# Softmax attention on one core: row sums moved into the maxima's PSUM banks, a third bank for scores, one maximum per instruction, and a new order within each tile

## The reference, cut to what matters

```python
out = softmax(q @ k_txt.T * SCALE, masked) @ v_txt + softmax(q @ k_img.T * SCALE) @ v_img
```

## Time and profile before

| | |
|---|---|
| time of the runs, median of 3 | 3357.7 us |
| time of the profiled execution | 3349.82 us |
| its span in the profile | 3347.8 us |
| attention, from the first score to the last `scale` | 906.7 to 2568.7 us |
| TensorE busy in the span | 3063.8 us (92%) |
| VectorE, ScalarE, GpSimd busy | 61%, 48%, 41% |

### The profile page before, as it was taken

How to read it: one execution, slowest core, us unless ns; L and a number is a source line. 1 busy time by engine, 2 the same in 40 slices (tenths; PEclk the granted TensorE clock), 3 DMA queues, 4 the chain that set the end, 5 groups by cost and what they waited for, 6 DMA issues and landing times. The chain is left out here.

```text
span 3347.8 us, 49752 instructions
## 1 busy us (share of the span) xinstructions
PE 3063.8 (92%) x15756; PEld 1888.5 (56%) x15756; DVE 2053.6 (61%) x3425; ACT 1606.9 (48%) x3005; POOL 1376.9 (41%) x545
## 2 busy tenths in 40 slices
PE   7999999999599999999999999999994488999991
PEld 6777777777344444444444444444441466777771
DVE  5666766666566666766766666667652774443435
ACT  3343433434166666666666666666663653222222
POOL 0000000000087787877877877778775161000000
PEclk9999999999599999999999999999996699999996
DMA  5666667676846466465565564664633361000005
GB/s 170 157 163 166 163 162 169 160 150 159 169 83 132 104 127 126 97 128 124 107 133 106 125 132 99 125 127 100 133 55 108 93 203 44 1 1 0 0 0 201
DMA packets 374881, 385.16 MB, mean 115 GB/s; under 512 B 47792, under 2 KB 297712, under 8 KB 368504
## 3 DMA queue, kind: packets, MB, share of 16 engines
q1 hardware_dynamic: 363272, 323.61, 40.7%
q0 software_dynamic: 7168, 50.34, 8.5%
q10 hardware_dynamic: 4224, 8.39, 0.7%
HBM read 210.77 MB, written 121.15 MB: 99 GB/s over the span
## 5 line engine op out<-in xcount | busy, mean ns | idle before, releaser
L962 ACT ACTIVATE at_probs<-at_st 128x512 f32<-128x512 f32 (+1 forms) x1664 | 914.0, 595 | 614.5 <-PE at_st L812 599.0
L992 DVE TENSOR_REDUCE at_cm<-at_mx 128x2 f32<-128x896 f32 x768 | 813.1, 1087 | 432.1 <-PE at_mx L828 432.1
L772 POOL TENSOR_TENSOR at_added<-at_added,at_probs 128x2048 f32<-128x2048 f32 x192 | 888.6, 4628 | 11.5
L812 PE MATMUL at_st<-at_qst,at_kst 101*128 101x512 f32 (+1 forms) x1664 | 656.0, 456 | 6.2 <-ACT at_probs L962 5.7
L812 PEld LDWEIGHTS at_st<-at_qst,at_kst 101*128 101x128 f32 (+1 forms) x1664 | 265.9, 184 | 597.4 <-ACT at_probs L962 454.1
L828 PE MATMUL at_mx<-at_kst,at_qst 97*128 97x448 f32 (+1 forms) x2048 | 530.1, 362 | 50.1 <-DMA at_kst<-stack_rows 23.2
L850 PE MATMUL at_acc<-at_probs,at_vt 128*32 128x512 f32 (+2 forms) x3584 | 478.3, 608 | 0.7 <-ACT at_probs L962 0.7
L828 PEld LDWEIGHTS at_mx<-at_kst,at_qst 97*128 97x128 f32 x2048 | 371.3, 194 | 158.6 <-DVE at_cm L992 77.4
L740 POOL MEMSET at_ones<- 128x32 f32 x1 | 0.1, 130 | 819.1 <-POOLq L302 819.1
L772 POOL TENSOR_TENSOR at_added<-at_probs 128x2048 f32<-128x2048 f32 x32 | 146.6, 4581 | 325.9 <-ACT at_probs L962 325.9
L1508 ACT ACTIVATE ff_h<-ff_psa,ff_b1c,alpha 128x512 f32<-128x512 f32 x128 | 99.5, 778 | 344.6 <-PE ff_psa L1485 344.6
(11 more groups left out here) (203 smaller groups left out, 4701.5 us busy)
## 6 DMA issues: line engine op xcount, KB each, us to landing
at_kst<-k_high SPq DMA_DIRECT2D x256, 200.0 KB
at_probs<-at_probs POOLq DMA_DIRECT2D x32, 1024.0 KB, 7.0
at_kst<-k_low SPq DMA_DIRECT2D x128, 200.0 KB
pj_xin<-in_ctx_dram SPq DMA_DIRECT2D x96, 256.0 KB, 4.2
k_high<-pj_kh SPq DMA_DIRECT2D x96, 256.0 KB, 3.1
k_low<-pj_kl SPq DMA_DIRECT2D x96, 256.0 KB, 4.7
values<-pj_vs SPq DMA_DIRECT2D x96, 256.0 KB, 4.6
at_vt<-values SPq DMA_DIRECT2D x32, 768.0 KB
```

What stands on the lines that cost most here:

```text
L772: pool.tensor_tensor(added[:], so_far, probs[:, SLOT[t]], ALU.add).then_inc(S["add_done"], 1)
L812: pe.matmul(st[0:kn, h % 2, :], kst[g.j][:, h, t * P:t * P + kn], qst[g.j][:, h, :], start=True, stop=True).then_inc(S["st_done"], 1)
L962: act.activation(probs[0:kn, SLOT[t], h, :], st[0:kn, h % 2, :], ACT.Exp, scale=SCALE).then_inc(S["exp_done"], 1)
L992: dve.tensor_reduce(dst, mx[:, 2 * slot:2 * slot + 2, 0:kn], AX.X, ALU.max, negate=last).then_inc(S["mx_free"], 1)
```

## The change

- `acc` has one bank (values); `st` has three, and a score waits for the exponential three earlier. Score number `(NST*j + HG*t + h)` modulo 3 gives the bank.
- The maxima are singles: each of the 64 matmuls has a bank of its own (its place in the group's list modulo 4) and a `tensor_reduce` of its own. A matmul waits for whatever used its bank last: a maximum's reduce, the copy of the tops, or the evacuation of a sum.
- The sums take places in the same list of banks. There are two, of two passes each: text (tile 6 and `added`) in tile 1 of the next group, image (tiles 12 and 11) in tile 2. The text half of tile 10 has no pass of its own: a third accumulating DMA adds it into `added`, behind all additions. Each fold has its own semaphore.
- In a tile the four scores come ahead of the values and the sums. Maxima stand between scores 2 and 3, behind score 3, and behind the values in the tiles without sums; at tiles 1 and 2 there are none behind the sums, and none in tile 10.
- 14 single maxima (before: five pairs) of group `g+2` are made in tiles 11 and 12. The ring's places are given out otherwise (`SLOT`).

The diff, cut to its core:

```diff
-    FOLDS = [(5, 0, P, 6), (10, HALF, P, 11)]
-    SUMMED = [(6, 0, P), (10, 0, HALF), (None, 0, P), (12, 0, KLAST), (11, 0, P)]
-    SUMS_AT = {10: [0], 11: [1]}
-    SUMS_LATE = {0: [2], 1: [3], 2: [4]}
+    FOLDS = [(5, 0, P, 6), (10, 0, HALF, None), (10, HALF, P, 11)]
+    SUMMED = [[(6, 0, P), (None, 0, P)], [(12, 0, KLAST), (11, 0, P)]]
+    SUMS_AFTER = {1: 0, 2: 1}
-    EARLY = 5
+    EARLY = 14
-    SLOT = [0, 1, 2, 3, 4, 5, 0, 1, 2, 3, 4, 5, 3]
+    SLOT = [0, 1, 2, 3, 0, 1, 2, 4, 5, 0, 3, 4, 5]
-        st, mx, acc = a.banks("st", 2), a.banks("mx", 4), a.banks("acc", 2)
+        st, mx, acc = a.banks("st", 3), a.banks("mx", 4), a.banks("acc", 1)
...
                 elif not g.first:
-                    pool.wait_ge(S["s_done"], NSUM * g.at(-1).G + SUM_IMG0)
+                    pool.wait_ge(S["s_done"], 2 * g.at(-1).G + 1)
...
             def body(g):
                 for n in range(NADD):
...
                     add(g, n)
+                fold(g, 1)
                 if not g.first:
                     scale(g.at(-1))
-                fold(g, 1)
+                fold(g, 2)
...
-                if not (g.first and t == 0 and h < 2):
-                    pe.wait_ge(S["exp_done"], n - 1)
-                pe.matmul(st[0:kn, h % 2, :], kst[g.j][:, h, t * P:t * P + kn], qst[g.j][:, h, :],
+                if not (g.first and t == 0 and h < 3):
+                    pe.wait_ge(S["exp_done"], n - 2)
+                pe.matmul(st[0:kn, bank, :], kst[g.j][:, h, t * P:t * P + kn], qst[g.j][:, h, :],
                           start=True, stop=True).then_inc(S["st_done"], 1)
...
+            def sums(g, q, bank):
+                if q == 0:
+                    pe.wait_ge(folded[0], 16 * (g.G + 1))
+                    pe.wait_ge(folded[1], 16 * (g.G + 1))
                     pe.wait_ge(S["add_done"], NADD * (g.G + 1))
+                else:
+                    pe.wait_ge(folded[2], 16 * (g.G + 1))
+                for k, (t, r0, r1) in enumerate(SUMMED[q]):
...
+                        done = pe.matmul(mx[cols, bank, :], ones[r0:r1, :], src, start=k == 0, stop=k == 1)
...
             def body(g):
                 for t in range(KT):
-                    for h in (0, 1):
+                    for h in range(HG):
                         scores(g, t, h)
                         ahead(g, t, h)
...
-                    for h in (2, 3):
-                        scores(g, t, h)
-                        ahead(g, t, h)
...
+                    if t in SUMS_AFTER and not g.first:
+                        n = place["sums", -1, SUMS_AFTER[t]]
+                        bank_free(g, n)
+                        sums(g.at(-1), SUMS_AFTER[t], n % 4)
                     ahead(g, t, "end")
...
-                dve.tensor_reduce(dst, mx[:, 2 * slot:2 * slot + 2, 0:kn], AX.X, ALU.max,
-                                  negate=last).then_inc(S["mx_free"], 1)
+                dve.tensor_reduce(dst, mx[:, bank % 4, 0:kn], AX.X, ALU.max, negate=last).then_inc(S["mx_free"], 1)
```

More of the change, by code:

```diff
@@ L627, in attend @@
     NCH = len(CH)
-    NPAIR = 2 * QT * NCH
+    NMAX = HG * QT * NCH
     NST = KT * HG
@@ L673, in attend, with spread @@
         plan = {}
[L674 to L680, removed]
-        spread(range(TOPS[0] + 1, KT), 2, range(EARLY))
+        def spread(tiles, step, singles):
+            places = [(t, at) for t in tiles for at in ((2, 3) if t in SUMS_AFTER else (2, 3, "end"))]
+            for n, m in enumerate(singles):
+                plan.setdefault(places[n * len(places) // len(singles)], []).append((step, m))
@@ new lines, in attend @@
+        spread(range(TOPS[0]), 1, range(EARLY, NMAX))
+        spread(range(TOPS[0] + 1, KT), 2, range(EARLY))
+        units = []
+        for t in range(KT):
+            for at in (*range(HG), "sums", "end"):
+                units += [("single",) + single for single in plan.get((t, at), [])]
+                if at == "sums" and t in SUMS_AFTER:
+                    units.append(("sums", -1, SUMS_AFTER[t]))
+        place = {unit: n for n, unit in enumerate(units)}
+        TOPS_AFTER = max(n for n, unit in enumerate(units) if unit[0] == "single" and unit[1] == 1)
@@ new lines, in runs, with bank_before @@
+        def runs(g, unit):
+            kind, step, _ = unit
+            return not (kind == "sums" and g.first) and g.followed(step)
+        def bank_before(g, n):
+            for body, top_n in ((g, n), (g.at(-1), len(units))):
+                known_start = body.known and body.G < 0
+                if known_start:
+                    there = [k for k in range(top_n) if units[k][:2] == ("single", 2)]
+                else:
+                    there = [k for k in range(top_n) if runs(body, units[k])]
+                there = [k for k in there if k % 4 == n % 4]
+                k = there[-1] if there else None
+                tops_between = top_n > TOPS_AFTER and (k is None or k <= TOPS_AFTER) and body.followed(1)
+                if tops_between:
+                    return ("tops", body.at(1), n % 4 // 2)
+                if k is not None:
+                    kind, step, m = units[k]
+                    return (kind, body.at(step), m)
+            raise ValueError("a bank without an earlier use")
@@ L683, in keys, with where @@
+        def where(m):
+            j, qt, kc, r = m // (2 * QT * NCH), m // (2 * NCH) % QT, m // 2 % NCH, m % 2
+            return 2 * j + r, qt, kc
         def keys(t):
@@ L914, in _ @@
                 values(g, q)
-            for q in range(SUM_IMG0 - 1, NSUM):
-                sums(g, q)
+            for q in range(2):
+                bank_free(g.at(1), place["sums", -1, q])
+                sums(g, q, place["sums", -1, q] % 4)
         @block.scalar
@@ L1016, in body @@
                 if not g.last:
-                    for m in range(0 if g.first else EARLY, NPAIR):
+                    for m in range(0 if g.first else EARLY, NMAX):
                         reduce(g.at(1), m)
@@ L1026, in _ @@
             dve.wait_ge(S["const_set"], NC)
-            for m in range(NPAIR):
-                reduce(Group(0, 0), m)
+            for m in range(NMAX):
+                reduce(Group(0, 0), m, True)
             negate(Group(0, 0))
```

126 lines of the change are left out of this document (62 added, 64 removed).

## The result

The changed kernel takes 3326.7 us (median of four, 3323.1 to 3327.5), beside 3358.0 for the kernel before: a ratio of 0.990 (95% interval 0.989 to 0.991). It is faster by some 31 us. I had forecast 3290, with 3237 to 3325 as the range: the sign was right, the gain half of what I said, and the time lies 2 us outside the range.

A forecast was written before the change was run, and what follows sets the result against it. Bound: a ring of GpSimd's additions, DMA into `added` and text sum, period 49.1 to 49.2 us against 51.24. Steady groups -61, start -5, first group -3, last +4: -65 us, so 3290 us, range 3237 to 3325.

The forecast's parts named there:

- the price of a single reduce: On VectorE: a single maximum costs 0.54 or 0.35 us, 64 of them 31.6 us a group, hidden.
- The sum of work: TensorE's own work in one group after the change, without waits: 45.1 us, from 47.1 before.
- The ring's terms: GpSimd's additions 38.2, issue of the DMA into `added` 0.7, its landing 8.0, text sum and release 2.2: 49.1 us.
- The waits of the two evacuations and of tile 3: TensorE waits behind ScalarE's evacuations: about 0.5 us each in tiles 1, 12 and 3.
- The margin of the other ring places: Places freed by GpSimd's additions 4 to 7 come in time for tiles 12 and 0: hidden, by 1 us.
- the one on scores: With three banks, score 3 waits for exponential 0 only in tile 10: 0.4 us a group.
- the tops: After tile 10's scores, the tops wait for the negation behind the last reduce: 0.6 us, 0.3 more than before.
- the ring through fold 1: GpSimd's additions, then the DMA into `added`, then TensorE's text sum, which releases the next additions: sets a 49.1 us period.
- The ends: Outside steady groups: -5 us ahead of the first group, about -3 in the first, +4 in the last.
- The clock: Rival, chance 0.07: TensorE's clock halves at the new wait; period 54.4 us, time near 3450 us.
- the later landing: Rival, chance 0.12: the DMA lands later or image-sum and place margins fail; period 50.3 to 51, 3320 to 3345 us.
- TensorE's list decides: Rival, chance 0.28: TensorE's own work and waits set the period, 47.9 or 47.0 us; 3228 to 3253 us.

The follow-up runs named there:

- the two-bank wait: Changed kernel, but a score waits for the exponential two scores earlier again, as with two banks: 3550.1 us, ratio 1.059.
- three small corrections: Changed kernel with three maxima between scores 2 and 3, evacuations one exponential later, tile 10's text half folded into tile 6: 3244.9 us, ratio 0.968.
- two and two scores: Changed kernel with tile order scores 0 and 1, values and sums, scores 2 and 3 again: 3442.1 us, ratio 1.027.

## Why the prediction was wrong

**Right.** What the parts save in work: the passes of sums, the changes between the two forms of matmul, the price of a single reduce, the 5.9 us at the start. The sum of work is 44.5 us a group where I had 45.1 (the period, less the waits below). The ring's terms: 38.3, 0.6, 8.0 measured for 38.2, 0.7, 8.0. The waits of the two evacuations and of tile 3: 1.45 us measured (intervals of tiles 1, 3 and 12 over their values without a wait) for 1.5. The margin of the other ring places.

**The step that failed** is the one on scores: "three scores and two maxima take 1.1. So it waits only where nothing stands between scores 2 and 3, in tile 10: 0.4". It is a term too small, in two ways. Exponential 0 starts 0.59, not 0.5, behind its score, so score 3 may start at 1.25 and reaches its place at 1.1; and any wait, however short, adds 0.1 for the weight load behind it. I had read that 0.1 for a maximum behind a wait and not applied it to a score. Adding the waits of score 3 over tiles 2 to 11 from the median intervals gives 2.3 us, and with the bare weight loads 3.3 instead of 0.4. (0.4 of it are in tile 11, where exponential 0 starts 1.06 behind its score, since ScalarE first copies the tops.) With 0.5 for VectorE in tile 0 (I had 0.3, for tiles 11 and 12), 0.15 for the tops (0.6), some 0.3 for the folds (none) and the 1.45 above, the waits are 5.7 us and not 2.8. The runs show it: three maxima in that place, with the folds out of the way, give 1.4 us, the two-bank wait costs 7.6, and with the evacuations and the fold together 2.3 are gained.

**A row read wrongly.** I had taken the 82.5 us of the kernel before for waits for exponentials and the 10.6 us for those on VectorE. As shown above, 63.7 of the 82.5 cost nothing. At 1805.05 the pair of scores took 1.10 where I had 0.46: 0.23 of the 0.64 are ahead of score 1, and 0.42 lie behind it, where the weight load of the first maximum waits for VectorE (1806.15 above). By the same intervals about half of the 4.1 us of waits were VectorE's, in four places of up to 0.5 us. So the third bank and the new order went for one half only and made more waits than they took; the single reduces went for the other.

**The bound.** I named the ring through fold 1, at 49.1. It does not bind in the changed kernel. Near it lies another one, through fold 2 and two groups, at 49.4. I had written that fold 2 "lands near 12 us after the last addition", free by 1 to 2 us; it lands after 2.4 + 12.3 = 14.7, since two folds in one queue beside SP's loads take 12.3 and not 8.3, as without fold 1. This costs 0.3 to 0.4 us a group here, and most of what the later evacuations gain.

**The ends.** The last group is 8.3 us longer, for 4 forecast; without fold 1 it is 2.7 longer. Its text sum waits 6.8 us for fold 1 and then runs at the half clock (0.50 granted from 2513.6 on), two passes in 3.6 us:

```profile
2525.92 1.93 PE L905 MATMUL at_mx<-at_probs,at_ones 128*32 128x512 f32 x8 [6.78 <-DMA at_added<-at_probs]
2527.60 1.96 PE L905 MATMUL at_mx<-at_added,at_ones 128*32 128x512 f32 x8
2531.10 3.64 PE L905 MATMUL at_mx<-at_probs,at_ones 65*32 65x512 f32 x16 [1.54 <-DMA at_probs<-at_probs]
```

**The rivals.** The clock did not fall in the changed kernel's steady groups. The measured time lies in the range of the later landing, 3320 to 3345, but by luck: a late fold was the smaller part of it, fold 2 and not fold 1, and TensorE's list the larger; the case "TensorE's list decides" was right in kind and I had its length wrong by 2.3 us. The range was made from the bounds of the ring and of that list, but the list's own terms had no bound above: 1.1 us against 1.1 us is no margin, and a place where two numbers meet needs both ends.

**Where the gain went.** One part of the change, the single reduces, is worth all that was measured. The saved pass and the fewer changes are worth 2 us more by the sums of work (the pass alone 0.9 to 1.3 by its run; no run undoes the changes of form alone), and the new order gives them back as waits of score 3.

## What to carry to other kernels

An instruction that is placed just where its input becomes ready is not hidden: count a short wait and the bare weight load in each repetition, and put one more independent matmul in front. A DMA that is issued last in a stage, beside the loads of the next, should be moved ahead of them, or given another target, before its duration is trusted. A wait listed for a weight load behind a pass of another form may cost nothing: lay the starts beside those of a place without a wait. Split a change into its parts on the chip: here one part of it was worth as much as the whole, and the rest paid only after three small corrections.

## What was not expected of the hardware

- **A wait bares the weight load.** 0.10 to 0.11 us for each, whatever its own length (0.34 instead of 0.23 behind a score that waited 0.14).
- **Two accumulating DMAs in one queue.** 512 KB land after 7.3 to 8.3 us (medians) when the one ahead in GpSimd's queue was issued 7 us earlier or more, and after 12.3 when it was issued 2 us earlier, beside SP's loads.
- **The clock falls after shorter gaps than I had allowed for.** With two and two scores, 1.2 GHz was granted after a stretch with TensorE busy for 4.71 of 6.0 us and a longest gap of 1.29 us, again and again: the granted clock from 1000 to 2400 us is 0.92 in the mean, which makes some 220 us at the half clock. I had taken one case of 3.24 us as the measure. The Trainium skill, "TensorE: Matmul & The Clock Gate", section "A second HAM failure mode", tells of short idle times between groups of matmuls that make the clock go back and forth; the trace agrees, with such a fall in each of the 30 groups of that kernel and in none of the changed one.
- **A reduce from PSUM, back to back,** costs 0.53 us for 448 elements (six in 3.27, one alone 0.62). By the Trainium skill, "VectorE: DVE Perf Modes", section "The TRN2 errata", an estimate is 0.59; the rows decide, and the start of the attention was 5.9 us shorter, not 2.
